# Decayed attention with a hand-written order: value products joined and placed two gaps later

## The reference

```
q = rope(x @ Wq.T); k = rope(x @ Wk.T); v = x @ Wv.T      # 16 heads, 4 shared k/v heads
for each chunk of positions:
    scores = (q @ k.T) * mask            # mask[t, s] = exp(-slope (t - s)) if t >= s else 0
    o  = scores @ v + (q * q_dec) @ kv   # inside the chunk + from the state
    kv = blk_dec * kv + (k * k_dec).T @ v
out = layernorm(x + o @ Wo.T)
```

## Time and profile before

| what | us |
|---|---|
| median of 3 runs (3271.25 to 3276.04) | 3272.31 |
| the profiled execution's own time | 3304.02 |
| its span | 3302.3 |
| busy: TensorE matmul, VectorE, ScalarE, GpSimd | 2769.0, 1988.6, 1299.1, 1074.4 |
| the decayed attention in the trace, some 730 us: same four | 618.9, 395.6, 144.9, 365.2 |

### The profile page before, as it was taken

How to read it: one execution, slowest core, us unless ns; L and a number is a source line. 1 busy time by engine, 2 the same in 40 slices (tenths; PEclk the granted TensorE clock), 3 DMA queues, 4 the chain that set the end, 5 groups by cost and what they waited for, 6 DMA issues and landing times. The chain is left out here.

```text
span 3302.3 us, 62960 instructions
## 1 busy us (share of the span) xinstructions
PE 2769.0 (84%) x17098; PEld 1958.3 (59%) x17099; DVE 1988.6 (60%) x3658; ACT 1299.1 (39%) x2735; POOL 1074.4 (33%) x1447
## 2 busy tenths in 40 slices
PE   5998999999899948868888888969888888819992
PEld 4575666667566637756666666644444444408992
DVE  3666656566665647855555555556666666536664
ACT  3554554545555512212222212215454444514443
POOL 4334253433434211125555555410111111122225
PEclk8999999999999979989999999979999999959996
DMA  2101111110111120130111110032222222043225
GB/s 62 40 24 43 37 30 37 27 43 24 43 34 27 33 79 32 38 112 27 32 32 32 32 29 22 26 86 63 64 64 64 59 59 58 22 140 108 72 74 196
DMA packets 146409, 175.43 MB, mean 53 GB/s; under 512 B 21130, under 2 KB 109730, under 8 KB 145570
## 3 DMA queue, kind: packets, MB, share of 16 engines
q1 hardware_dynamic: 135076, 149.89, 15.7%
q0 software_dynamic: 6912, 18.96, 1.5%
q10 hardware_dynamic: 4224, 4.19, 0.4%
HBM read 90.83 MB, written 37.06 MB: 39 GB/s over the span
## 5 line engine op out<-in xcount | busy, mean ns | idle before, releaser
L560 ACT ACTIVATE soft_probs<-soft_ps_s,soft_mx 128x512 f32<-128x512 f32 x512 | 347.9, 685 | 395.4 <-DVE soft_mx L479 371.1
L479 DVE TENSOR_REDUCE soft_mx<-soft_ps_s 128x1 f32<-128x512 f32 x512 | 329.3, 685 | 236.8 <-PE soft_ps_s L389 224.2
L1807 DVE TENSOR_REDUCE mla_mx<-mla_ps_s 128x1 f32<-128x512 f32 x512 | 337.9, 686 | 188.0 <-PE mla_ps_s L1660 154.5
L1918 ACT ACTIVATE mla_pt<-mla_ps_t 128x512 f32<-128x512 f32 x512 | 292.6, 597 | 328.9 <-PE mla_ps_t L1672 302.8
L389 PE MATMUL soft_ps_s<-soft_ks,soft_qs 128*128 128x512 f32 x1024 | 309.9, 422 | 13.0 <-ACT soft_probs L560 13.0
L398 PE MATMUL soft_ps_p<-ident,soft_probs 128*128 128x128 f32 x2048 | 266.7, 273 | 12.1 <-DVE soft_mx L479 6.6
L398 PEld LDWEIGHTS soft_ps_p<-ident,soft_probs 128*128 128x128 f32 x2048 | 236.8, 141 | 47.1 <-DVE soft_mx L479 8.3
L489 DVE COPY soft_pt<-soft_ps_p 128x512 f32<-128x512 f32 x256 | 175.5, 686 | 137.7 <-PE soft_ps_p L398 130.0
L389 PEld LDWEIGHTS soft_ps_s<-soft_ks,soft_qs 128*128 128x128 f32 x1024 | 171.1, 190 | 146.9 <-issue 58.9
L1660 PE MATMUL mla_ps_s<-mla_stack,mla_pad 128*128 128x512 f32 x512 | 242.3, 480 | 12.0 <-DVE mla_mx L1807 6.4
L407 PE MATMUL soft_ps_a<-soft_pt,soft_v 128*64 128x512 f32 x1024 | 251.5, 613 | 0.0
(11 more groups left out here) (359 smaller groups left out, 6678.1 us busy)
## 6 DMA issues: line engine op xcount, KB each, us to landing
soft_rrep<-inverse SPq DMA_DIRECT2D x128, 128.0 KB, 2.9
mla_pad<-mla_stack SPq DMA_DIRECT2D x256, 64.0 KB, 2.0
moe_xt<-by_expert SPq DMA_DIRECT2D x72, 129.0 KB, 2.1
soft_ks<-soft_ks SPq DMA_DIRECT2D x64, 128.0 KB, 2.3
decay_ks<-decay_ks SPq DMA_DIRECT2D x64, 128.0 KB, 2.4
raw<-in_L_ffn_w SPq DMA_DIRECT2D x16, 512.0 KB, 8.2
mla_stack<-mla_yh SPq DMA_DIRECT2D x128, 64.0 KB, 2.1
soft_xc<-in_L_attn_x SPq DMA_DIRECT2D x8, 512.0 KB, 4.3
```

The costliest lines, as they stand in the source:

```text
L479: op = vv.tensor_reduce(out=mx[:, h, t:t + 1], in_=ps_s[:, s_bank(4 * h + t), :], axis=AX.X, op=ALU.max, negate=True)
L560: op = nc.scalar.activation(probs[:, h % 2, t, :], ps_s[:, s_bank(4 * h + t), :], ACT.Exp, bias=mx[:, h, t:t + 1], scale=1.0, accum_out=rs ...
L1807: op = vv.tensor_reduce(out=mx[:, a, t, s:s + 1], in_=ps_s[:, (16 * a + 4 * t + s) % S_BANKS, :], axis=AX.X, op=ALU.max, negate=True)
L1918: op = nc.scalar.activation(pt[:, t % 2, s, :], ps_t[:, s % 2, :], ACT.Exp, scale=KPH ** -0.5)
```

## The change

The two value steps of a block are made together, in the gap at+5 and not at+3 and at+4, next to IN. What depends on them (HA, LA, TM, OA) goes one gap later, the state's steps VD, KV2 and KH of groups 2 and 3 two gaps later, W one or two gaps later. EPS, RSTD, N and ST follow closer on W. Nothing is added or taken out: every step stays, with its operands.

```diff
@@ -705,25 +705,25 @@
         for u, (at, back) in {("KV", 0): (2, 7), ("KV", 1): (3, 8), ("Q", 0, 0): (5, 9), ("Q", 0, 1): (7, 11), ("KV", 2): (9, 13), ("KV", 3): (11, 14),
                               ("Q", 0, 2): (13, 16), ("Q", 0, 3): (15, 18), ("Q", 1, 0): (17, 20), ("Q", 1, 1): (19, 22), ("Q", 1, 2): (21, 24), ("Q", 1, 3): (22, 26)}.items():
             project(at, u, back)
-        put(10, "gpsimd", ("VV", 0)); put(15, "gpsimd", ("VV", 1))
-        for g, at in enumerate((12, 14, 22, 25)):
+        put(10, "gpsimd", ("VV", 0)); put(16, "gpsimd", ("VV", 1))
+        for g, at in enumerate((12, 14, 24, 27)):
             put(at, "vector", ("VD", g)); put(at + 1, "tensor", ("KV2", g)); put(at + 1, "scalar", ("KH", g))
         for b, (g, c) in enumerate(blocks):
             at = S0 + 3 * b
             for n in range(3):
                 put(at + n, "tensor", ("S", g, c, n)); put(at + n + 1, "vector", ("M", g, c, n))
             for q in range(2):
-                put(at + 3 + q, "tensor", ("A", g, c, q))
+                put(at + 5, "tensor", ("A", g, c, q))
             if c == 0:
-                put(at + 5, "scalar", ("HA", g, 0)); put(at + 5, "vector", ("LA", g, 0))
+                put(at + 6, "scalar", ("HA", g, 0)); put(at + 6, "vector", ("LA", g, 0))
             else:
-                put(at + 4, "tensor", ("IN", g)); put(at + 5, "vector", ("TM", g), ("OA", g))
-                put(at + 6, "scalar", ("HA", g, 1)); put(at + 6, "gpsimd", ("LA", g, 1))
+                put(at + 5, "tensor", ("IN", g)); put(at + 6, "vector", ("TM", g), ("OA", g))
+                put(at + 7, "scalar", ("HA", g, 1)); put(at + 7, "gpsimd", ("LA", g, 1))
         put(ROUND + 1, "sync", ("LX",)); put(ROUND + 2, "sync", ("LB",))
-        for t, at in enumerate((34, 36, 41, 43)):
+        for t, at in enumerate((35, 37, 43, 45)):
             put(at, "tensor", ("W", t, 0)); put(at + 1, "tensor", ("W", t, 1))
-            put(at + 1, "vector", ("F", t), ("B", t), ("G", t)); put(at + 2, "gpsimd", ("EPS", t), ("RSTD", t))
-            put(at + 3, "vector", ("N", t)); put(at + 4, "sync", ("ST", t))
+            put(at + 1, "vector", ("F", t), ("B", t), ("G", t)); put(at + 1, "gpsimd", ("EPS", t), ("RSTD", t))
+            put(at + 2, "vector", ("N", t)); put(at + 2, "sync", ("ST", t))
 
         S, ahead, order = {}, {}, {}
         turn = {"T": 0, "QT": 0, "KT": 0, "A": 1, "KV2": 1, "IN": 1, "W": 2, "S": 3, "Q": 4, "KV": 4}
```

## The result

The changed kernel takes 3306.20 us, median of 4 runs (3300.11 to 3307.51), the kernel before 3273.3 us (4 runs); the ratio is 1.0094, with a 95% interval of 1.0081 to 1.0108. The difference is +33 us; forecast were +31 and 3303.

A forecast was written before the change was run, and what follows sets the result against it. TensorE was nearest to the bound, busy 75.4 of 85.8 us per batch, the rest waits. Terms summed to +4.7 per batch, +33 over seven, -2 in the last: +31, 3335 profiled, 3303 unprofiled; range 3276 to 3326.

The forecast's parts named there:

- Part 1, visits: TensorE's visits to 64-column products in decayed attention fall from 17 to 11 per batch, 0.4 us each: -2.4 us.
- Part 2, waits removed: TensorE's waits, mostly value products A for masks M, all taken off: -10.0 us per batch, an upper bound.
- Part 3, gap 5: S.3.0.1 waits for M, delayed because Y.KV.0 must wait for the later KV2.3 to read kr: +5.2 us per batch.
- Boundary: Between batches, QT.1.2.0 waits for ROT.Q.1.3's bank and QT.1.2.1 for XL.0: +5.2 us per batch.
- The last batch: The eighth batch has no next projections, so neither long wait; five joined visits there give -2 us.
- Four smaller ones: New TensorE waits in gaps 9, 15, 17 and 18 of 1.2, 1.5, 0.9 and 1.5 us: +5.1 per batch.
- Gap 17: S.1.0.1 needs M behind ROT.Q.0.3, 2.2 us against 1.3 of cover: +0.9 us per batch.
- Clock: Two low-clock stretches per batch instead of one, behind the two long waits: +1.6 us; bounds 0 and +4.8.
- rival B: The clock stays low longer after each long wait, +3.2 us per batch: 3325 us; chance 15%.
- D: Rival: the gap 5 wait does not form, one clock fall as today, -2.1 us per batch: 3256 us; 10%.
- C: Rival: no change, since the four small waits don't form, -36 us against the forecast: 3267 us; 8%.
- E: Rival: score steps S take over A's waits one for one, no new waits, only visits saved: 3254 us; 4%.

The follow-up runs named there:

- joined kernel: The kernel before with only the joining: both value products of a block made together at at+4, nothing else moved; 3249.30 us, ratio 0.9925.
- W early: The changed kernel with output projection W and its dependents (F, B, G, EPS, RSTD, N, ST) one gap earlier; 3296.83 us, ratio 1.0075 to the kernel before.
- KV2.3 early with masks first: The changed kernel with KV2.3 back in gap 2 and M ahead of TM and OA on VectorE; 3270.93 us, ratio 0.9991 to the kernel before.
- all repairs: The changed kernel with KV2.3 in gap 2, A.0.1 in gap 23, M ahead of TM and OA, W one gap earlier; 3245.55 us, 0.9910 to before.
- halves apart: The changed kernel with the first half of the value products one gap earlier (at+4), the second at at+5; 3290.57 us, ratio 1.0052 to the kernel before.

## Why the prediction was right, step by step

The mechanism was right: A's waits went, and two long and four smaller waits came where they were forecast. The sum is nearer than its terms, and that is partly luck: the visits saved 1.2 us less per batch than forecast, the boundary cost 1.2 less.

| term, us per batch | predicted | measured |
|---|---|---|
| visits, six fewer | -2.4 | -1.2 |
| waits of before taken off | -10.0 | -10.2 |
| gap 5, S.3.0.1 | +5.2 | +5.04 |
| boundary, QT.1.2 | +5.2 | +3.99 |
| gap 9, QT.0.0.1 | +1.2 | +0.6 |
| gap 15, KV2.1 | +1.5 | +1.35 |
| gap 17, S.1.0.1 | +0.9 | +1.55 |
| gap 18, QT.0.3.0 | +1.5 | +1.25 |
| clock | +1.6 | some +2.2 |
| sum | +4.7 | +4.5 |

The visits and the clock are not read directly: with waits and half of the low-clock time taken off, a period is 73.8 us before and 72.6 in those periods of the changed kernel in which little of the low clock lies beside a wait; the clock's term is what then is missing to 4.5.

*Part 1, visits:* the mechanism held, the size was double. The prices at the seams of single instructions add up to more than a visit costs in the stream; which of them is too high no run separates.

*Part 2, waits removed:* right, A waits no longer. That S would take over was right too, as the joined kernel shows.

*Part 3, gap 5:* right in place, cause and size, to 0.2 us. Counted from the end of KV.0's issue (1718.73), Y starts at 5.65 (forecast 5.75), ROT at 8.17 (8.3) and S.3.0.1 at 11.16 (11.25). Joined products ahead of KV.1, KV2.3 behind it, Y held, ROT.KV.1, then VC, TM, OA, M: each step is in the rows.

*Boundary:* the place and the two waits (for ROT's bank, for XL) were right; the size was 1.2 us too high. Counted from the end of Q.1.2's issue, XL.0 ends at 10.8 and not at 11.3, since N.3 was 0.54 long and not 0.9; and TensorE needs 6.9 us for its own work up to QT.1.2.1, not 6.1. What failed is a reason: "F.3, now ahead of ROT.Q.1.2" is no cause, as W early showed. The chain got longer by it, and TensorE's cover by W.3.1 as well.

*The last batch:* forecast -2 us, measured about +1.7. The stage is 32.8 us longer in all; the six periods are 26.9 of it, one more period 4.5, the start -0.4. "Neither long wait" was wrong for the boundary: Q.1.3 of the last batch is made one batch ahead, so its ROT is late here too, and with no T in front TensorE waits longer for it:

```profile
2158.46 1.06 PE L874 MATMUL decay_ps_m<-ident,decay_st 128*128 128x128 f32 x8 [3.16 <-DVE decay_rt L979]
```

*Four smaller ones:* all appeared. Gap 9 was half the forecast, and why stays open: the products made slow by the low clock behind gap 5 are not the reason, since the wait is 0.60 us as well in the two kernels whose clock is high there (KV2.3 early with masks first, and all repairs). Gap 17 was larger, for a wait that I had put at nothing: "GpSimd issues EPS and RSTD behind LO as before". For t = 1 both stand in gap 14 before and after, and N.1 stands ahead of ROT.Q.0.3 in both. But LA.2.1 has moved from gap 13 to gap 14, between LO.Q.0.2 and EPS.1 on GpSimd, and takes 1.29 us there. In the changed kernel N.1 waits 4.06 us for RSTD.1:

```profile
1673.57 0.69 DVE L1003 TENSOR_TENSOR decay_pt<-decay_ps_s,decay_near 128x512 f32<-128x512 f32 x1
1678.33 0.41 DVE L1038 TENSOR_SCALAR decay_xb<-decay_xb,decay_mv,decay_rstd 128x256 f32<-128x256 f32 x1 [4.06 <-POOL decay_rstd L1139]
1678.66 1.22 DVE L979 TENSOR_TENSOR decay_rt<-decay_ps_m,decay_rope 128x1024 f32<-128x1024 f32 x1
```

```profile
1674.68 1.27 POOL L1119 TENSOR_TENSOR decay_st<-decay_rt,decay_st 128x512 fp32r<-128x512 f32 x1 [0.18 <-POOL decay_st L1116]
1675.91 1.29 POOL L1130 TENSOR_TENSOR decay_atl<-decay_ot,decay_ath 128x512 fp32r<-128x512 f32 x1
...
1677.73 0.57 POOL L1139 TENSOR_TENSOR decay_rstd<-decay_vare,minus_half 128x1 f32<-128x1 f32 x1 [0.34 <-POOL decay_vare L1134]
```

In the kernel before it waits 1.97 us:

```profile
1664.59 0.67 DVE L1038 TENSOR_SCALAR decay_xb<-decay_xb,decay_mv,decay_rstd 128x256 f32<-128x256 f32 x1 [1.97 <-POOL decay_rstd L1139]
```

```profile
1662.15 1.30 POOL L1119 TENSOR_TENSOR decay_st<-decay_rt,decay_st 128x512 fp32r<-128x512 f32 x1 [0.18 <-POOL decay_st L1116]
...
1663.98 0.57 POOL L1139 TENSOR_TENSOR decay_rstd<-decay_vare,minus_half 128x1 f32<-128x1 f32 x1 [0.34 <-POOL decay_vare L1134]
```

ROT.Q.0.3 starts at 1678.66, when N.1 is through, and S.1.0.1 behind it pays. W early bears this out: RSTD.1 comes ahead of LO.Q.0.2 there, N.1 doesn't wait, and the wait in gap 17 is 0.66.

*Clock:* the place was right (a low stretch behind each of the two long waits, or from shortly before its end), and the sum came near the forecast; rival B, longer low stretches, is true in half of the batches: the clock is low for 13.6 us in all there, of which some 3 lie inside the waits, and these periods are 91.1 us long against 89.8 for those with short low stretches.

*Rivals:* D fell with the 5.04 us in gap 5, C with the four small waits, E with all of them. E's first half, S in A's place, is what the joined kernel does.

## What to carry to other kernels

Moving a step later in a hand-written order must be priced at every buffer that it frees: KV2.3 was the last reader of kr, and its two gaps became 2.4 us of the 5 that the next batch waits in gap 5. A wait is the other engine's cadence less the work in front of it; so look at what work leaves a stretch with the step that you move, as joined products do better in the gap where the half already stood. When one edit joins, delays and rearranges, time the parts alone: here the joining was worth 25 us and the rest cost 58.

## What the runs showed of the hardware

A visit to products of 64 weight columns among those of 128 costs 0.2 us in this stream by the joined and the changed kernel, 0.3 by the one with halves apart; the single rows had suggested 0.4. The prediction's estimate from the drain in the Trainium skill ("TensorE: Matmul & The Clock Gate", Step-by-step) was 0.11. That it is the number of columns that costs, and not the change to another kind of product as such, no run shows. The granted clock fell to its lower level behind waits of 2 to 5 us in one or two pieces, or towards their end, in some batches and not in others of the same kernel, and stayed there while the engine was fully busy. Over six batches it was low for 10.8 us per batch in the changed kernel, whose waits are the longest, so that a wait can cost more than its length. But the sum of the waits doesn't set it: the clock was low for 1.1 us where they are 8.0 or 8.9, for 2.8 where they are 7.3, and for 3.4 where they are 11.0. Why, stays open. And one execution of an unchanged stage took 31.6 us (5%) longer than in the profile of the changed kernel, as its score products show above; its cause stays open.
